# Attention scores from fp16 halves in place of fp32, with PSUM copies, expert weights and statistics in another order

## The reference, cut to what matters

```python
hidden = gelu(x @ down_W.T + down_b)                  # per sequence
hidden = (hidden @ Wsel.T + bsel) + domain_emb[idx]   # the sequence's expert
x = layernorm(hidden @ up_W.T + up_b + x) * ln_gamma + ln_beta
x = ln(x) * (1 + scale) + shift                       # from the timestep
q, k, v = x @ Wq + bq, x @ Wk + bk, x @ Wv + bv
scores = (q / sqrt(32)) @ k.T + attention_bias        # 16 heads, 512 x 512
probs = softmax(where(src_mask, -inf, scores))
x = x + (probs @ v) @ Wo + bo
```

## Time and profile before

| | |
|---|---|
| median of 3 runs | 2879.29 us (2878.21 to 2886.77) |
| profiled execution | 2890.35 us, span 2888.5 us |
| granted PE clock, mean | 0.954 |
| PE busy | 2518.5 us, 87% |
| DVE busy | 2065.3 us, 72% |
| ACT busy | 1155.1 us, 40% |
| POOL busy | 1207.8 us, 42% |

### The profile page before, as it was taken

The page is one execution under the profiler, slowest core; times in us unless marked ns, Lnnn a source line. Parts: engine busy times, 40 slices in busy tenths (PEclk is TensorE's granted clock), DMA queues, the critical chain, the costliest instruction groups (busy, mean ns, idle before and its releaser), DMA issues.

```text
span 2888.5 us, 46383 instructions
## 1 busy us (share of the span) xinstructions
PE 2518.5 (87%) x14115; PEld 1212.6 (42%) x14203; DVE 2065.3 (72%) x3845; ACT 1155.1 (40%) x2197; POOL 1207.8 (42%) x1024
## 2 busy tenths in 40 slices
PE   3788888888888888884999999999999999999992
PEld 1344444444444444442444444444444444444440
DVE  4575757676666757576886777868788687886877
ACT  2464656564565646463332222323223232232221
POOL 3553444445353535352433424334343343433426
PEclk8899999999999999997999999999999999999995
DMA  4443443344344333334422222222232222322222
GB/s 128 138 132 130 132 137 125 130 132 130 117 142 120 132 130 120 130 130 147 133 98 79 93 98 99 91 84 93 92 107 90 81 91 91 110 87 88 86 70 80
DMA packets 155669, 319.39 MB, mean 111 GB/s; under 512 B 17714, under 2 KB 23474, under 8 KB 155458
## 3 DMA queue, kind: packets, MB, share of 16 engines
q1 hardware_dynamic: 145666, 299.13, 31.4%
q10 hardware_dynamic: 9792, 17.83, 1.7%
HBM read 298.85 MB, written 17.86 MB: 110 GB/s over the span
## 4 chain that ended last, share of the span: by engine, by line
PE 37%; issue 7%; DVE 5%; POOL 4%; ACT 1%; DMA 0%; SPq 0%; DVEq 0%; POOLq 0%; ACTq 0%
PE ffn_bank L1330 11%; PE ffn_bank L1331 11%; PE ffn_bank L1332 11%; POOL prod L1251 2%; PE ffn_bank L1323 2%; POOL f L1241 1%; POOL x L1269 1%; PE ffn_bank L1389 1%; PE ffn_bank L1339 0%; DVE tmp L1532 0%; DVE g2T_hi L1623 0%; ACT g L1451 0%; DVE tmp L1572 0%; DVE g2T_lo L1624 0%; DMA b<-in_b 0%
## 5 line engine op out<-in xcount | busy, mean ns | idle before, releaser
L756 ACT ACTIVATE tiles<-tiles,nmax 128x512 f32<-128x512 f32 x512 | 365.4, 715 | 322.7 <-DVE nmax L938 322.6
L938 DVE CUSTOM_DVE_ANT_0 tiles<-bank,bias 128x512 f32<-128x512 f32 x512 | 326.5, 685 | 106.8 <-PE bank L591 100.7
L488 POOL TENSOR_TENSOR bias<-bias,mask_add 128x1024 f32<-128x1024 f32 x128 | 271.6, 2132 | 216.2 <-DMA bias<-in_bias 206.0
L614 PE MATMUL bank<-ident,tiles 128*128 128x128 f32 x2048 | 283.7, 281 | 83.0 <-ACT pT L737 36.4
L1623 DVE CAST g2T_hi<-g 128x512 f16<-128x512 f32 x256 | 189.4, 740 | 156.5 <-ACT g L1451 151.6
L614 PEld LDWEIGHTS bank<-ident,tiles 128*128 128x128 f32 x2048 | 220.1, 141 | 165.6 <-issue 72.8
L1624 DVE TENSOR_TENSOR g2T_lo<-g,g2T_hi 128x512 f16<-128x512 f32 x256 | 269.9, 1054 | 8.8
L950 DVE COPY pT<-bank 128x512 f32<-128x512 f32 x256 | 174.4, 689 | 115.6 <-PE bank L614 115.6
L1451 ACT ACTIVATE g<-ffn_bank,bi 128x512 f32<-128x512 f32 x128 | 88.0, 687 | 362.3 <-PE ffn_bank L1332 328.4
L1251 POOL TENSOR_TENSOR prod<-grid,f 128x512 f32<-128x512 f32 x108 | 165.5, 1559 | 131.6 <-DMA grid<-in_grids 125.5
L1330 PE MATMUL ffn_bank<-w_hi,g2T_hi 128*128 128x512 f16 x512 | 197.0, 385 | 25.0 <-DVE g2T_lo L1624 24.7
(11 more groups left out here) (256 smaller groups left out, 5180.3 us busy)
## 6 DMA issues: line engine op xcount, KB each, us to landing
bias<-in_bias SPq DMA_DIRECT2D x256, 512.0 KB, 4.1
raw<-in_W_l SPq DMA_DIRECT2D x128, 512.0 KB, 3.3
grid<-in_grids SPq DMA_DIRECT2D x172, 256.0 KB, 3.5
xin<-in_x SPq DMA_DIRECT2D x36, 256.0 KB, 4.0
x2n<-x_rows SPq DMA_DIRECT2D x9, 1024.0 KB, 7.0
out<-outt ACTq DMA_DIRECT2D x36, 256.0 KB, 2.0
x_rows<-tiles ACTq DMA_DIRECT2D x32, 256.0 KB, 2.9
l_rows<-in_rows SPq DMA_DIRECT2D x8, 768.0 KB, 4.4
```

The source lines that it names most:

```text
L488: pool.tensor_tensor(bias[:, n % NB, :, :], bias[:, n % NB, :, :], mask_add[:, u % T, :].unsqueeze(1).to_broadcast([P, 2, S]), ALU.add).th ...
L614: mm = pe.transpose(bank[:, t * P:(t + 1) * P], tiles[:, 4 * (u % NR) + i, t * P:(t + 1) * P], ident[:, :])
L756: act.activation(tile, tile, ACT.Exp, scale=-1.0, bias=nmax[:, u % 2, i:i + 1], accum_out=rsum[:, j, h:h + 1]).then_inc(prob_ready, 1)
L938: dve.tensor_tensor_reduce(tiles[:, 4 * (u % NR) + i, :], bank[:, :], bias[:, half % NB, i % 2, :], -1.0, 3.0e38, ALU.add, ALU.min, nmax[: ...
```

## The change

The scores are computed from fp16 halves of q and k. ACT makes the hi halves of both, DVE computes the scaled value again from the bank into `qk32` and subtracts hi. PE runs three rounds of four products (hi hi, hi lo, lo hi), each head on its 32 rows. Around it the order changes:
- the projection of the second block of v moves from slot 0 to the loop's head;
- the expert weights move from the loop's head to the end of slot 1 on DVE;
- T0 and T1 are copied by DVE, T2 and T3 by ACT, each after the slot's four tiles; `TAKEN_AFTER` says after how many exps ACT takes the `BESIDE` results;
- DVE makes reciprocals and `rinv_x` ahead of the `BESIDE` results and turned tiles; PE spreads them after the values;
- the context's lower half moves from slot 4g + 7 to 4g + 8;
- statistics run in pairs at the ends of slots 6, 7, 11 and 12, ACT's scalings at the ends of slots 9, 10 and 14; POOL's root and gains come later by two slots, for the second norm after all mask adds.

```diff
-BESIDE = {0: [("v", 1), ("xT", 0), ("xT", 1)], 1: [("v", 2), ("xT", 2), ("xT", 3)],
+BESIDE = {0: [("xT", 0), ("xT", 1)], 1: [("v", 2), ("xT", 2), ("xT", 3)],
           2: [("v", 3), ("down",), ("q", 1)], 3: [("expert",), ("k", 1)], 4: [("up", 0), ("up", 1)],
-          5: [("R", 0), ("up", 2), ("up", 3)], 6: [("q", 2)], 7: [("k", 2)], 9: [("R", 1)], 10: [("q", 3)],
+          5: [("up", 2), ("up", 3), ("R", 0)], 6: [("q", 2)], 7: [("k", 2)], 9: [("R", 1)], 10: [("q", 3)],
           11: [("k", 3)], 13: [("R", 2)], 17: [("R", 3)]}
-ACT_L0 = {33 + t: ("scale0", t) for t in range(T)} | {49 + t: ("scale1", t) for t in range(T)}
-DVE_L0 = {24 + t: ("stats0", t) for t in range(T)} | {40 + t: ("stats1", t) for t in range(T)}
+TAKEN_AFTER = {1: 3, 2: 3, 3: 3, 6: 2, 7: 2, 10: 2, 11: 2}
+ACT_L0 = {9: (("scale0", 0), ("scale0", 1)), 10: (("scale0", 2), ("scale0", 3)),
+          14: tuple(("scale1", t) for t in range(T))}
+DVE_L0 = {1: (("expert_weights",),), 6: (("stats0", 0), ("stats0", 1)), 7: (("stats0", 2), ("stats0", 3)),
+          11: (("stats1", 0), ("stats1", 1)), 12: (("stats1", 2), ("stats1", 3))}
...
@@ PE, scores
-                    for i in range(4):
-                        rows = slice(HD * i, HD * i + HD)
-                        pe.matmul(psum[i][:, :], q32[rows, g, j * P:(j + 1) * P], k32[rows, g, :],
-                                  start=i < 2, stop=True).then_inc(full[i], 1)
+                    for part, (w, x) in enumerate(((0, 0), (0, 1), (1, 0))):
+                        for i in range(4):
+                            rows = slice(HD * i, HD * i + HD)
+                            mm = pe.matmul(psum[i][:, :], q16[w][rows, g, j * P:(j + 1) * P], k16[x][rows, g, :],
+                                           start=part == 0 and i < 2, stop=part == 2)
+                            if part == 2:
+                                mm.then_inc(full[i], 1)
...
@@ DVE, take
-                    if name == "k":
+                    if name in ("q", "k"):
...
+                        dve.wait_ge(at_hi, it * C + m + 1)
+                        if name == "k":
+                            dve.wait_ge(q_split, it * C + m + 1)
+                        link(dve.tensor_scalar(qk32[:, :], bank[:, :], scale, b[:, m:m + 1], ALU.mult, ALU.add))
+                        dve.tensor_tensor(lo[:, m, :], qk32[:, :], hi[:, m, :], ALU.subtract).then_inc(split, 1)
...
@@ DVE, one slot, after the four scorings and the reciprocals
+                    for key in BESIDE.get(u, []):
+                        take(key)
+                    if 0 < u <= NQ:
+                        for i in (0, 1):
+                            bank = arrived(dve, it, ("T", u - 1, i))
...
                         if u == 4 * g + 6:
                             context(g)
-                        if u == 4 * g + 7 and g < G - 1:
+                        if u == 4 * g + 8 and g < G - 1:
                             context_lo(g)
+                    for part in DVE_L0.get(u, ()):
+                        l0_part(link, it, part)
```

More of the change, by code:

```diff
@@ L124, in attention_pass @@
 def attention_pass(nc, a, ada_rows, x2_dram):
-    order = [(("q", 0), 4), (("k", 0), 5), (("v", 0), 6)]
+    order = [(("q", 0), 4), (("k", 0), 5), (("v", 0), 6), (("v", 1), 7)]
     order += attention_slots()
@@ L164, in attention_pass @@
         xT = [sb(f"xT_{h}", [P, C, S], F16) for h in ("hi", "lo")]
-        q32 = sb("q32", [P, C, S], F32)
-        k32 = sb("k32", [P, C, S], F32)
+        q16, k16 = ([sb(f"{n}16_{h}", [P, C, S], F16) for h in ("hi", "lo")] for n in "qk")
+        qk32 = sb("qk32", [P, S], F32)
         v32 = sb("v32", [P, T, D], F32)
@@ L491, in _ @@
                         up_bias(it)
-                    if u == 8:
+                    if u == 10:
                         rstd_of_norm(base, it + 1, 0)
[L494 to L502, removed]
+                    if u in (11, 12):
+                        gain(it, base, 0, 2 * u - 22)
+                        gain(it, base, 0, 2 * u - 21)
+                rstd_of_norm(base, it + 1, 1)
+                pool.wait_ge(ada_in, it * 16 + 32)
+                for t in range(T):
+                    gain(it, base, 1, t)
         @block.tensor
@@ L628, in _ @@
                 pe.wait_ge(x1T_split, it * C + C)
-                for key in (("q", 0), ("k", 0), ("v", 0)):
+                for key in (("q", 0), ("k", 0), ("v", 0), ("v", 1)):
                     project(key)
@@ L645, in _ @@
                         values(v, kb)
+                    for g in range(G):
+                        if ("R", g) in BESIDE.get(u, []):
+                            spread(g)
                     if 0 < u <= NQ:
@@ L711, in take @@
                     name, m = key[0], key[-1]
-                    if name == "q":
+                    if name in ("q", "k"):
+                        hi, scale, b, ready = {"q": (q16[0], 1.0 / (WS * math.sqrt(HD)), bq, q_hi),
+                                               "k": (k16[0], 1.0 / WS, bk, k_hi)}[name]
                         bank = arrived(act, it, key)
-                        act.activation(q32[:, m, :], bank[:, :], ACT.Identity, scale=1.0 / (WS * math.sqrt(HD)),
-                                       bias=bq[:, m:m + 1]).then_inc(q32_ready, 1)
+                        act.activation(hi[:, m, :], bank[:, :], ACT.Identity, scale=scale,
+                                       bias=b[:, m:m + 1]).then_inc(ready, 1)
                     elif name == "v":
@@ L727, in _ @@
                 take(("q", 0))
+                take(("k", 0))
                 take(("v", 0))
+                take(("v", 1))
                 def context_hi(g):
@@ L737, in evacuate @@
                     act.activation(pT[:, (u // 2) % 2, i, :, (u % 2) * P:(u % 2 + 1) * P],
-                                   bank[:, :].rearrange("p (t q) -> p t q", t=T), ACT.Copy).then_inc(pT_ready[0], 1)
+                                   bank[:, :].rearrange("p (t q) -> p t q", t=T), ACT.Copy).then_inc(pT_ready[1], 1)
                 for u in range(SLOTS_ALL):
-                    places = TURNED.get(u, (1, 3))
                     for i in range(5):
-                        n = 4 * u + i
-                        if i == min(3, places[0]):
+                        if i == TAKEN_AFTER.get(u, 4):
                             for key in BESIDE.get(u, []):
                                 take(key)
[L747 to L752, removed]
+                        if i < 4 and u < NQ:
                             tile = tiles[:, 4 * (u % NR) + i, :]
                             h, j = 4 * (u // T) + i, u % T
-                            act.wait_ge(scored, 1 + it * HT + n + 1)
+                            act.wait_ge(scored, 1 + it * HT + 4 * u + i + 1)
                             act.activation(tile, tile, ACT.Exp, scale=-1.0, bias=nmax[:, u % 2, i:i + 1],
                                            accum_out=rsum[:, j, h:h + 1]).then_inc(prob_ready, 1)
[L758 to L762, removed]
+                    if 0 < u <= NQ:
+                        for i in (2, 3):
+                            evacuate(u - 1, i)
+                    for part in ACT_L0.get(u, ()):
+                        l0_part(it, part)
+                    for g in range(G - 1):
+                        if u == 4 * g + 7:
+                            context_hi(g)
                 for c in range(2):
@@ L922, in context_lo @@
                         .then_inc(ctx_split, 1)
+                take(("q", 0))
                 take(("k", 0))
@@ L940, in _ @@
                                 .then_inc(scored, 1)
[L941 to L951, removed]
                     for g in range(G):
```

42 lines of the change are left out of this document (24 added, 18 removed).

## The result

The changed kernel takes 2914.56 us, median of four runs (2907.82 to 2922.63), against 2878.75 (2877.41 to 2886.77) for the kernel before: 1.0113 of its time, 95% interval 1.0094 to 1.0131. The prediction was 2868, range 2838 to 2898: the sign is wrong and the time lies outside.

What follows compares the result with a forecast made beforehand. PE leads in the attention pass (busy 1054 of 1225 us) but is not the only limit. Slot terms of -0.85 and -0.6 for the clock, times 8 rounds, give -11.6: 2879.3 to 2868 us, range 2838 to 2898.

Steps and rivals of the forecast that it cites:

- Loop head: Start of each round: scores start sooner despite subtractions waiting for POOL's adds, -2.0 us (-0.8 -0.95 -0.3).
- tail: End of each round: ACT scalings delay exps, but no rinv_x wait ahead of the output products, -0.6 us.
- Score block: PE's score products each slot: 0.65 us in fp16, PE gaining 0.42 a slot; DVE starts 1.1 after the block starts.
- the slower 0.84: Score block on PE: estimate by the skill page's four-strip speedup instead of 0.65, 3 us a round more at worst.
- Slots 4 to 14: Middle of the round: 4, 8, 12 and 14 longer, 6 and 10 shorter; forecast lengths sum to 78.3 us.
- The 0.7 of port waits charged to slots 10 and 11: Slots 10 and 11: subtractions beside POOL's gains were each charged 0.7 us extra.
- Slots 0 to 2 (+0.4): Expert weights end slot 1, 3.5 us, delaying slot 2's scoring by 1.9 against 2.4 of slack: +0.4 us.
- Slot 3 (+0.5): DVE does e, then k's lower half, then tile 0: 8.9 us for 8.4, +0.5.
- The clock (-0.6): Stretches at 1.2 GHz make other rounds 2.4 us longer; slower PE partly hidden, a quarter taken: -0.6 a round.
- Rival 1: Slower by shared ports: every new subtraction meets POOL, charged 1.2 us each; +26, 2893 us; chance 0.27.
- the second rival: Another name for Rival 1, used where the prediction cites the rule on two SBUF inputs; chance 0.27.
- the sign of being wrong that it named: The new DVE subtractions averaging over 1.3 us would show the forecast wrong.

Runs made afterwards that it cites:

- e6: The changed kernel with fp32 scores and the expert weights in slot 2 behind the four scorings: 2831.43 us, 0.9824 of the kernel before.
- e7: e4 with ACT writing scale and bias back into the bank and DVE making the low half by one subtraction from it, no qk32: 2828.61 us, 0.9809.
- e8: e6 with reciprocals and rinv_x moved below DVE's copies of tiles 0 and 1: 2823.63 us, 0.9794 of the kernel before.
- e9: e7 with reciprocals and rinv_x behind DVE's copies, as in e8: 2833.95 us, 0.9828 of the kernel before.
- e11: e8 with turned tiles 0 and 2 copied by ACT again, and ACT taking slots 9 and 13 results after two exps: 2881.93 us, 0.9993.
- e10: e9 with turned tiles 0 and 2 copied by ACT again, and ACT taking slots 9 and 13 results after two exps: 2909.59 us, 1.0095.
- e12: The kernel before, old order, with fp16 halves, ACT writing scale and bias back into the bank and DVE's low half from the bank: 2891.43 us, 1.0031.
- e4: The changed kernel with the expert weights in slot 2 behind the four scorings: 2881.28 us, 1.0001 of the kernel before.
- e3: The changed kernel with the expert weights back at the loop's head: 2906.01 us, 1.0097 of the kernel before.
- e2: The changed kernel with fp32 scores and all of the new order: 2867.98 us, 0.9945 of the kernel before.
- e5: The changed kernel with the low halves subtracted from the PSUM bank, bias left out, qk32 still made but unread: 2879.63 us, 0.9982.

## Why the prediction was wrong

- **Loop head: right.** Scores follow a wait of 1.85 for 6.09; q's and k's subtractions took 1.88 and 1.61 in the round shown, as the working with POOL's adds had it; tail and head gain 1.9 together, forecast 1.4 (-0.8 and -0.6; the other 1.25 of the head's term lies in slot 0).
- **Score block: right** (0.22 per group, DVE 1.10 behind it); the slower 0.84 that the prediction held possible did not come. But the block is worth nothing at the end: e6 and e7 agree within their intervals, and in the three other pairs of orders (e8 and e9, e11 and e10, before and e12) the kernel with halves is the slower by 0.3, 1.0 and 0.3%.
- **Slots 4 to 14: right in sum and nearly each.** The long forms of 4, 8, 12 and 14, the short 6 and 10, and that `rinv_x` would take 0.43, all came. The 0.7 of port waits charged to slots 10 and 11 didn't.
- **Slots 0 to 2 (+0.4): the first failed step.** With the head's 1.25 in slot 0 the forecast was -0.85 for these three; they grew by 1.8. Slot 0 lost 2.8 and slot 1 gained 2.0, near the forecast together; the miss is in slot 2, +2.6. The working gave the expert weights 3.5 us and slot 2 a slack of 2.4. They took 5.5: I took one of the five operations as held up, and POOL's adds, back to back for 9 us, held two; the cast in slot 2 (0.43 at best) then took 1.97. e4 prices the place at 1.0113 - 1.0001, 33 us; the move from the head had brought nothing (e3).
- **Slot 3 (+0.5): the second.** k's subtraction was taken at 0.69. It meets POOL's add, and takes 2.23; slot 3 grew by 2.5. POOL's add waits for a bias load that DVE's second scoring of the slot releases, and in the eight slots 3 it comes 4.7 to 5.1 us after the first scoring: 603.05 + 5.0 = 608.0 in the one shown, where the subtraction starts at 608.46. "By the bias loads its adds fall at slot starts, the subtractions in the middle" held for k's subtraction in slots 7 and 11 (0.69 and 0.8) and failed here.
- **The clock (-0.6): wrong sign.** The pass has 0.95 for 0.96. Slot 3 runs partly at 1.2 GHz behind the 3.55 wait. I had let longer chains hide the clock; the longer waits stand ahead of the stretches in which it is low. But the clock isn't what makes slot 3 long: its granted clock, as a mean over the eight rounds, is 0.84 in the change and 0.83 in e2, where slot 3 lasts 9.5 for 11.7, and 0.89 in e4, where it lasts 11.3.
- **Rival 1 had the mechanism, not the sizes.** It put the time at 2893, 26 above the forecast; measured is 47 above. (The prediction calls it "the second rival" in one place.) The rule of the Trainium skill, "SBUF — State Buffer", section "Who interferes with whom", that a DVE instruction with two SBUF inputs is locked out while GpSimd reads SBUF, is borne out: L917 took up to 2.4 with two SBUF inputs and 0.69 in all 64 cases with one in PSUM. The same section counts `tensor_scalar`, under conditions on its operands, among those that can contend with GpSimd; L838, from SBUF to SBUF, agrees (2.03 for 0.23). The rival let every subtraction wait 1.2, 9.6 a round; I had counted 3.1 of that by guessing phases. Measured is 3.1, so the forecast's total was right, and the sign of being wrong that it named, subtractions over 1.3 on average, did not show (1.08). What failed is where the waits lie: half of them in slot 3, on a bank that PE needs, and another 3.9 a round in the expert weights, of which the forecast had counted half and the rival left the rest out.

Each cause by itself is as large as the loss: e4 takes back 33 us and e5 38, of 36. That is no contradiction, since the change also holds a gain: its order alone is worth 11 to 16 us (e2). The two edits have not been run together; e7, which frees the ports and places the weights, and takes one DVE operation per tile away besides, is 86 under the change.

## What to carry to other kernels

Before a DVE operation is added, ask where its operands lie. Here a subtraction with one operand in a PSUM bank took 0.69 beside POOL or not, and one with both operands in SBUF was held until 0.55 us after POOL's 2.1-us add, up to 2.4 in all. Small operations suffer most for their size: five of 128 columns went from 5.5 to 1.6 us by standing where POOL is idle and DVE waits. A total of waits isn't enough for a forecast; what counts is which of them stands in front of a bank that PE needs. The cheaper product on PE gained nothing in any order tried here; and an order can be good (0.9945) and a datatype neutral (e6 against e7) where the two together lose 1.1%.

## What the runs showed that I had not expected

- DVE work moved to ACT did not show as a loss: e7 adds an ACT operation of 0.65 (`bank<-bank`, in place in PSUM) per q and k tile, and the round is 6.3 us shorter than e4's. How much of that is the port and how much the DVE operation saved isn't separated.
- Halves alone in the old order cost 3%, more than twice the whole change; the reordering was what made them nearly bearable.
- e11: engine order matters beyond the slot. The same copies on another engine cost 58 us, most of it in slots 5 and 2; the rows show how for slot 5, and slot 2 stays open.
